# A decoder layer on one core: residuals added in PSUM by an identity matmul, and the first batch's gate projection placed later

## The chip, the cores and the metric

One core of a Trainium2 chip runs the whole program. The metric is the device time of one execution in microseconds (us), where less is better. Times come from repeated runs and from one profiled execution.

## The reference, cut to what matters

The layer works on x of 32 batches x 256 tokens x 256 features. It has three mixers, each followed by a residual and a layer norm. All arithmetic is float32.

```
x = layernorm(x + ssm(x))          # d_inner 512, 16 states, conv of 3 taps
x = layernorm(x + cross_attn(x))   # 16 heads of 16, keys and values from ctx
x = layernorm(x + experts(x))      # 8 experts, d_ff 704, SiLU gate

# ssm, per batch:
xc, res = split(x @ W_in.T + b_in)
u = silu(causal_conv(xc) + conv_b)
dlt, Bm, Cm = split(u @ W_x.T)
delta = softplus(dlt @ W_dt.T + b_dt)
state = exp(delta * A) * state + delta * Bm * u   # a scan over each chunk of 64 tokens
y = sum over states(state * Cm) * silu(res)       # silu(res) is the gate
return y @ W_out.T + b_out
```

## The kernel before

The program has two parts. `mixers` computes the first two layer norms for the 32 batches, `experts` the third. The change touches only `mixers`.

Each engine has its own program, written out by a software pipeline, `run_steps`. A batch's work is cut into pieces, and each piece has an offset. An iteration of the pipeline has 16 slots. A piece with offset o runs in slot o mod 16, and it works on the batch that is o // 16 behind the newest. Within a slot an engine runs its pieces in the order in which its list has them. So in one iteration the convolution of one batch, the scan of the batch before it and the attention of two to five batches before it are interleaved, and an engine that waits in one piece holds up all pieces behind it.

The names that the prediction uses, with the slot of each piece before the change:

- `conv(m)`, m = 0 to 3, on TensorE in slots 1, 3, 5 and 7: the input projection and the convolution, six matmuls of 128x256 from `w_conv`. The PSUM bank `a_ps` holds two of the four blocks, and a bias matmul opens the bank. `conv_evac` on ScalarE (slots 4 and 8) copies the bank to `u`.
- `gate_proj(m)` on TensorE in slots 2 and 6 (bank `f_ps`), and `gate_evac` on ScalarE.
- `silu` on ScalarE (slot 9): a table load, SiLU of `u`, SiLU of the gate, and a second table load. Then `x_proj` (slot 9), `xp_evac`, `dt_proj` (slot 10), `softplus` (slot 11), and on GpSimd `w_piece`, the product of u and delta (slot 12). `delta` and `w` go to DRAM and come back replicated over the partitions.
- The scan: `dBu_piece(t)` on GpSimd, `decay(t, half)` on ScalarE, `scan(t, half)` on VectorE, for 16 tiles t, one per slot. Three `dBu` buffers and three PSUM banks `dA_ps` couple the engines. Some products with C run on GpSimd (`hC_piece`, L516), some on VectorE (L777, followed by `clear_starts`, a small memset, L787, which releases the buffers).
- `state_sum(m)` on TensorE in slots 5, 9, 13 and 1 (bank `y_ps`), after the `hC` products; `gating(m)` on VectorE.
- `out_proj` on TensorE (slot 4) and `attn_out` (slot 0), both into `a_ps`. `residual` on VectorE (slots 5 and 1): one 128x512 add (L804), two `bn_stats` (L807), two aggregations (L813). `norm` on ScalarE (slots 5 and 2).
- The attention, with one head per slot: `scores` and `row_max`; `scores_T` and `softmax_exp`. `head_transpose` on TensorE is in slots 15, 3, 7 and 11, and on its list it stands behind `conv`. `head_norm` on VectorE (L849, L854) is in slots 0, 4, 8 and 12, between the two scans of its slot.

Nine pieces share `a_ps` besides the convolution: `x_proj`, half of `dt_proj`, the projections of q and k, `out_proj`, `attn_out` and three transposes. `Bank.wait_read` makes TensorE wait until the last reader of the bank is done:

```
def wait_read(self, eng):
    if self.last:
        sem, count = self.last
        eng.wait_ge(sem, count)
```

Of the kernel before, what the change touches and what calls it, by code (L numbers as in the profile page):

```python
# [10 lines left out]
ALU = mybir.AluOpType  # L11
# [3 lines left out]
P = 128  # L15
# [4 lines left out]
ND = DI // P  # L20
# [20 lines left out]
NDA = 3  # L41
# [152 lines left out]
def mixers(nc, io, x2_dram, scratch, shared):  # L194
# [3 lines left out]
    with ExitStack() as ctx:  # L198
# [75 lines left out]
        def scores_T_bank(n):  # L274
# [4 lines left out]
        s_const = sem("weights_loaded")  # L279
        s_const_p = sem("const_set_pool")  # L280
# [18 lines left out]
        s_r1, s_st1, s_mv1, s_ln1 = sem("residual1"), sem("stats1"), sem("moments1"), sem("ln1_steps")  # L299
# [15 lines left out]
        s_r2, s_st2, s_mv2, s_ln2 = sem("residual2"), sem("stats2"), sem("moments2"), sem("ln2_steps")  # L315
# [14 lines left out]
        N_CONV = 6 + NDA + TAPS * KD  # L330
# [7 lines left out]
        def _(sp):  # L338
            sp.dma_start(w_xc.rearrange("p q t -> p (q t)"), io["w_xc"]).then_inc(s_conv_ld, 16)
            sp.dma_start(conv_rows, io["conv_rows"].partition_broadcast(P)).then_inc(s_conv_ld, 16)  # L340
            for tile, name in bias_parts:
                sp.dma_start(tile, io[name]).then_inc(s_bias_ld, 16)
# [184 lines left out]
        def _(act):  # L527

            nc.scalar.preload_act_table_set(EXP_LN)
            act.wait_ge(s_bias_ld, 16 * len(bias_parts))  # L530
            nc.scalar.activation(a_neg[:], a_neg[:], ACT.Exp).then_inc(s_const_a, 1)
# [16 lines left out]

            def silu(b):
                act.wait_ge(s_conv, b.value(2, 2))  # L550
                nc.scalar.activation(u[:], u[:], ACT.Silu).then_inc(s_u, 1)
                act.wait_ge(s_gate, b.value(2, 2))
                nc.scalar.activation(gate[:, b.par], gate[:, b.par], ACT.Silu).then_inc(s_gsilu, 1)
                nc.scalar.preload_act_table_set(EXP_LN)

# [33 lines left out]
            def norm(i, s_mv, s_steps, s_x):  # L589
                def piece(b):  # L590
# [101 lines left out]
            def max_load(gr):  # L692
# [11 lines left out]
                *[(O_GATE + 4 * half + 2, gate_evac(half)) for half in range(2)],  # L704
# [20 lines left out]
        def _(dve):  # L725
            nc.vector.memset(xT[:, :, 0:TAPS - 1], 0.0).then_inc(s_const_v, 1)
            nc.vector.memset(eps, EPS).then_inc(s_const_v, 1)
            for i in range(NDA):
                nc.vector.memset(dA[i][:], 0.0).then_inc(s_const_v, 1)
            dve.wait_ge(s_conv_ld, 32)  # L730
# [700 lines left out]
```

## Time and profile before

| | |
|---|---|
| median of 3 runs | 2796.05 us (2788.73 to 2799.86) |
| the profiled execution | 2792.28 us |
| its span, first to last instruction | 2790.5 us |
| busy share TensorE / VectorE / ScalarE / GpSimd | 87% / 77% / 65% / 74% |
| mean granted TensorE clock | 0.955 of full speed |

The span has three stretches. The first 71 us prepare constants and bring batch 0 to its scan. The 32 scans follow, until about 2190 us, and the experts take the rest, with GpSimd idle. Busy shares over the whole span mix these stretches, so the rows below look into one of them at a time. In the timelines, a float32 matmul appears as two instructions, so "x12" is six matmuls.

### The profile page before, as it was taken

To read this page: it belongs to the slowest core of one execution; us is meant where nothing else is said; L and a number is where in the kernel's file an instruction comes from. 1 tells how busy PE (TensorE), PEld (TensorE's weight loads), DVE (VectorE), ACT (ScalarE), POOL (GpSimd) and SP (SyncE) were. 2 spreads that over 40 slices of the span, in tenths; PEclk is the share of its full clock that TensorE was granted. 3 is DMA by queue.
4 is the path that set the end of the run, shared out by engine and by line. 5 is a ranking of instruction groups with operands and counts; after the bars stand their busy time and mean duration, and the time that the engine had idled before them with its cause. 6 is when DMAs were issued, how large, how long until landed. Compare 5 with 4: busy or idle time off the path is not lost. (4 is left out here: it accounts for less than half of the span.)

```text
span 2790.5 us, 49779 instructions
## 1 busy us (share of the span) xinstructions
PE 2424.6 (87%) x14816; PEld 1660.6 (60%) x14816; DVE 2140.0 (77%) x3586; ACT 1802.9 (65%) x3972; POOL 2074.5 (74%) x968
## 2 busy tenths in 40 slices
PE   3578888888889898889889888898888879999998
PEld 2345666666666666666666666666665545555554
DVE  1778999999999999999999999999999832322332
ACT  1666777877888888777877787878777541211111
POOL 2999999999999999999999999999999500000000
PEclk8788999999999999999999999999998879999999
DMA  3456566666666666666666666666666360343221
GB/s 118 128 133 149 150 165 168 165 158 157 157 169 166 160 158 165 165 162 168 166 169 164 162 164 166 165 173 163 166 172 158 86 180 12 91 126 96 78 79 31
DMA packets 319323, 399.65 MB, mean 143 GB/s; under 512 B 115697, under 2 KB 256241, under 8 KB 314962
## 3 DMA queue, kind: packets, MB, share of 16 engines
q1 hardware_dynamic: 303698, 384.91, 53.5%
q10 hardware_dynamic: 15360, 11.55, 1.5%
q8 instruction: 124, 2.03, 0.3%
q14 instruction: 141, 1.16, 0.2%
HBM read 300.86 MB, written 94.37 MB: 142 GB/s over the span
## 5 line engine op out<-in xcount | busy, mean ns | idle before, releaser
L506 POOL TENSOR_TENSOR arena<-arena 128x1024 f32<-128x1024 f32 x512 | 1208.2, 2363 | 66.6 <-DMA arena<-w_dram 42.3
L582 ACT ACTIVATE dA_ps<-arena,a_neg 128x252 f32<-128x252 f32 x2048 | 868.7, 461 | 330.4 <-DVE dA_ps L787 172.0
L764 DVE TENSOR_TENSOR_SCAN arena<-dA_ps,arena 128x512 f32<-128x512 f32 x672 | 803.6, 1208 | 112.5 <-ACT dA_ps L582 88.0
L516 POOL TENSOR_TENSOR arena<-arena 128x1024 f32<-128x1024 f32 (+1 forms) x416 | 808.1, 1943 | 17.8 <-DVE arena L764 17.2
L764 DVE TENSOR_TENSOR_SCAN dA_ps<-dA_ps,arena 128x512 f32<-128x512 f32 x352 | 416.2, 1205 | 3.9 <-POOL arena L506 3.7
L887 PE MATMUL a_ps<-xT,w_conv 128*128 128x256 f32 x1536 | 369.8, 391 | 0.0
L829 DVE TENSOR_REDUCE mx<-s_ps 128x2 f32<-128x512 f32 x497 | 334.0, 672 | 23.2 <-PE s_ps L887 23.2
L887 PEld LDWEIGHTS a_ps<-xT,w_conv 128*128 128x128 f32 x1536 | 288.4, 194 | 54.1 <-issue 16.5
L887 PE MATMUL y_ps<-arena,sel 128*32 128x256 f32 x4096 | 257.5, 393 | 55.5 <-DVE m_rows L835 27.8
L640 ACT ACTIVATE probs<-st_ps 128x512 f32<-128x512 f32 x493 | 285.3, 579 | 29.7 <-PE st_ps L887 25.5
L887 PE MATMUL s_ps<-k_st,q_st 96*128 96x256 f32 x994 | 260.6, 344 | 43.7 <-DVE mx L829 28.0
L887 PE MATMUL st_ps<-q_st,k_st 96*128 96x256 f32 x986 | 221.9, 307 | 51.5 <-ACT probs L640 41.8
L777 DVE TENSOR_TENSOR arena<-dA_ps,arena 128x512 f32<-128x512 f32 x352 | 230.9, 677 | 4.4
L887 PEld LDWEIGHTS st_ps<-q_st,k_st 96*128 96x128 f32 x986 | 154.1, 194 | 120.1 <-issue 100.3
L887 PEld LDWEIGHTS s_ps<-k_st,q_st 96*128 96x128 f32 x994 | 166.7, 197 | 98.0 <-issue 59.4
L887 PEld LDWEIGHTS y_ps<-arena,sel 128*32 128x32 f32 x4096 | 127.9, 112 | 144.2 <-POOL arena L516 64.9
L1240 DVE TENSOR_TENSOR hT<-silu,u_ps 128x512 f32<-128x512 f32 x80 | 55.0, 688 | 193.7 <-PE u_ps L1311 160.9
L887 PE MATMUL a_ps<-bias 2*128 2x512 f32 (+2 forms) x192 | 93.3, 486 | 117.4 <-DVE parts L819 38.4
L1213 ACT ACTIVATE silu<-g_ps 128x512 f32<-128x512 f32 (+1 forms) x96 | 56.5, 596 | 210.0 <-PE g_ps L1311 209.9
L1311 PE MATMUL g_ps<-arena 128*128 128x512 f32 x384 | 181.7, 599 | 3.1 <-PEq L198 3.1
L1311 PE MATMUL u_ps<-arena 128*128 128x512 f32 x320 | 150.5, 592 | 0.0
L1329 PE MATMUL d_ps<-arena,hT 128*128 128x256 f32 x640 | 145.9, 383 | 0.0
(111 smaller groups left out, 3272.9 us busy)
## 6 DMA issues: line engine op xcount, KB each, us to landing
arena<-delta_dram SPq DMA_DIRECT2D x512, 128.0 KB, 2.8
arena<-w_dram SPq DMA_DIRECT2D x512, 128.0 KB, 3.2
arena<-bc_dram SPq DMA_DIRECT2D x128, 256.0 KB, 4.5
q_st<-q_parts_dram SPq DMA_DIRECT2D x512, 64.0 KB
k_st<-k_parts_dram SPq DMA_DIRECT2D x512, 64.0 KB
w_dram<-u SPq DMA_DIRECT2D x32, 512.0 KB, 2.8
delta_dram<-delta SPq DMA_DIRECT2D x32, 512.0 KB, 3.8
k_parts_dram<-parts SPq DMA_DIRECT2D x32, 512.0 KB, 4.0
```

The source lines that it names most:

```text
L506: pool.tensor_tensor(dBu[:, n % NB], w_r[:, n // RP % 2, t % RP].unsqueeze(1).to_broadcast([P, QS, L]), bc_r[:, b.par, 0], ALU.mult).then_ ...
L516: pool.tensor_tensor(h[:, n % NH, states], h[:, n % NH, states], bc_r[:, b.par, 1, states], ALU.mult).then_inc(s_hC, 1)
L582: last = nc.scalar.activation(dA[n % NDA][:, q, :, 1:], delta_r[:, n // (2 * RP) % 2, t % RP].rearrange("p (c t) -> p c t", t=CH)[:, :, 1: ...
L640: nc.scalar.activation(probs[:, n % NPROB], scores_T_bank(n), ACT.Exp, scale=float(DK) ** -0.5).then_inc(s_exp, 1)
L764: nc.vector.tensor_tensor_scan(dst, decays, dBu[:, n % NB, 2 * half:2 * half + 2].rearrange("p q t -> p (q t)"), 0.0, ALU.mult, ALU.add).t ...
L777: nc.vector.tensor_tensor(h[:, n % NH, 2 * half:2 * half + 2], state[:].rearrange("p q c t -> p q (c t)"), bc_r[:, b.par, 1, 2 * half:2 * ...
L829: nc.vector.tensor_reduce(mx[:, hd], scores_bank(b.value(H, hd)), AX.X, ALU.max).then_inc(s_max, 1)
L887: return nc.tensor.matmul(out, lhsT, rhs, start=first, stop=last)
L1213: nc.scalar.activation(dst, g_ps[i % 2][first:last], ACT.Silu).then_inc(f_silu, 1)
L1240: nc.vector.tensor_tensor(hT[first:last, i // 2, HALF * (i % 2):HALF * (i % 2 + 1)], silu[first:last, i % 2], ups[first:last], ALU.mult).t ...
L1311: ins = nc.tensor.matmul(ps[i % 2][:], w13[:, b.par, k, col:col + P], x2T[:, b.par, k, cols], start=(k == 0), stop=(k == KD - 1))
L1329: nc.tensor.matmul(d_ps[(2 * t + i) % ND_PS][:, 0:D], hT[:, k, tokens], w2[:, b.par, k], start=(k == 0), stop=False)
```

## The change

1. The two residual adds leave VectorE. After the matmuls of `out_proj` and of `attn_out`, TensorE multiplies the identity by the tokens' x and accumulates into the same bank: one 128x256 matmul per 128 tokens, so two for each projection. `bn_stats` and the normalisation read the sum from `a_ps`, no longer from SBUF.
2. The bank `a_ps` is therefore released by the last read of `norm` on ScalarE, where it was released by the add.
3. `conv(0)` moves on TensorE from slot 1 to slot 3, and `conv(2)` from slot 5 to slot 7. Each bank of the convolution is now opened and filled in one slot.
4. For batch 0 only, the gate projection moves behind `dt_proj`, and its copies and SiLU behind `softplus`. `x_proj` waits for three weights that are loaded first.
5. At the start, the bias rows are loaded ahead of the convolution weights, and ScalarE copies them instead of VectorE.

```diff
-            (w_gate[:], "w_gate"), (w_x[:], "w_x"), (w_dt[:], "w_dt"), (sel[:], "sel"), (w_out[:], "w_out"),
+        front_weights = [(w_x[:], "w_x"), (w_dt[:], "w_dt"), (w_gate[:], "w_gate")]
...
+            for tile, name in bias_parts:
+                sp.dma_start(tile, io[name]).then_inc(s_bias_ld, 16)
             sp.dma_start(w_xc.rearrange("p q t -> p (q t)"), io["w_xc"]).then_inc(s_conv_ld, 16)
...
             def load_weights():
+                for tile, name in front_weights:
+                    sp.dma_start(tile, io[name]).then_inc(s_front, 16)
+                sp.wait_ge(s_const_v, N_SET)
                 for tile, name in weights:
                     sp.dma_start(tile, io[name]).then_inc(s_const, 16)
-                    sp.wait_ge(s_const_v, N_SET)
...
+            act.wait_ge(s_const_v, N_ROWS)
+            nc.scalar.activation(bias[:], rows, ACT.Copy).then_inc(s_const_a, 1)
...
+            def silu_gate(b):
+                act.wait_ge(s_gate, b.value(2, 2))
+                nc.scalar.activation(gate[:, b.par], gate[:, b.par], ACT.Silu).then_inc(s_gsilu, 1)
+
             def silu(b):
                 act.wait_ge(s_conv, b.value(2, 2))
                 nc.scalar.activation(u[:], u[:], ACT.Silu).then_inc(s_u, 1)
-                act.wait_ge(s_gate, b.value(2, 2))
-                nc.scalar.activation(gate[:, b.par], gate[:, b.par], ACT.Silu).then_inc(s_gsilu, 1)
+                if b.back(1):
+                    silu_gate(b)
                 nc.scalar.preload_act_table_set(EXP_LN)
+
+            def first_gate(b):
+                if not b.back(1):
+                    for half in range(2):
+                        gate_evac(half)(b)
+                    silu_gate(b)
+                    nc.scalar.preload_act_table_set(EXP_LN)
...
-                        nc.scalar.activation(xt[:, b.c % NX, tt], xt[:, b.c % NX, tt], ACT.Identity, bias=shift[:, i, tt:tt + 1],
+                        nc.scalar.activation(xt[:, b.c % NX, tt], a_ps[:, tt], ACT.Identity, bias=shift[:, i, tt:tt + 1],
                                              scale=rstd[:, i, tt:tt + 1]).then_inc(s_x, 1)
...
-                *[(O_GATE + 4 * half + 2, gate_evac(half)) for half in range(2)],
+                *[(O_GATE + 4 * half + 2, later_gate_evac(half)) for half in range(2)],
+                (O_SP + 2, first_gate),
...
-            def residual(i, s_mm, src_ps, s_r, s_st, s_mv, s_steps, s_in, per_batch):
-                def piece(b):
-                    r = xt[:, b.c % NX]
+            def moments(i, s_mm, s_st, s_mv, s_steps):
+                def piece(b):
                     dve.wait_ge(s_mm, b.value(TT, TT))
-                    dve.wait_ge(s_in, b.value(per_batch, per_batch))
-                    nc.vector.tensor_tensor(r, src_ps[:], r, ALU.add).then_inc(s_r, 1)
-                    dve.wait_ge(s_r, b.value(1, 1))
                     for tt in range(TT):
-                        nc.vector.bn_stats(st[:, i, tt], r[:, tt]).then_inc(s_st, 1)
+                        nc.vector.bn_stats(st[:, i, tt], a_ps[:, tt]).then_inc(s_st, 1)
...
+            def first_gate(b):
+                if not b.back(1):
+                    for m in range(ND):
+                        gate_proj(m)(b)
...
             def x_proj(b):
+                if not b.back(1):
+                    pe.wait_ge(s_front, 16 * len(front_weights))
+                    pe.wait_ge(s_const_v, N_SET)
...
                     for k in range(ND):
-                        i = mm(a_ps[:, tt, :], g[:, k, tt * P:(tt + 1) * P], w_out[:, k], False,
-                               tt == TT - 1 and k == ND - 1)
-                    i.then_inc(s_out_mm, 1)
-                    bank_a.read_by(s_r1, 1, b, 1)
+                        mm(a_ps[:, tt, :], g[:, k, tt * P:(tt + 1) * P], w_out[:, k], False, False)
+                    if tt == 0:
+                        pe.wait_ge(s_xtok, b.value(16, 16))
+                    mm(a_ps[:, tt, :], ident[:], x_of(b)[:, tt], False, tt == TT - 1).then_inc(s_out_mm, 1)
+                    bank_a.read_by(s_x1, TT, b, TT)
...
+                    mm(a_ps[:, tt, :], ident[:], x_of(b)[:, tt], False, tt == TT - 1).then_inc(s_of_mm, 1)
+                    bank_a.read_by(s_x2, TT, b, TT)
...
-                *[(O_CONV + 2 * m, conv(m)) for m in range(ND)],
-                *[(O_GATE + 4 * (m // 2), gate_proj(m)) for m in range(ND)],
+                *[(O_CONV + 2 + 4 * (m // 2), conv(m)) for m in range(ND)],
+                *[(O_GATE + 4 * (m // 2), later_gate(m)) for m in range(ND)],
+                (O_SP + 1, first_gate),
```

**The first place** is TensorE's program in slots 3 and 4 of an iteration in the middle of the run. `s_ps` and `st_ps` are `scores` and `scores_T`, and `f_ps<-ident,oT` is `head_transpose`. Before:

```order
L887 MATMUL s_ps<-k_st,q_st 128x256 x2
L887 MATMUL st_ps<-q_st,k_st 128x256 x2
L887 MATMUL a_ps<-xT,w_conv 128x256 x6
L1084 MATMUL f_ps<-ident,oT 128x128 x2
L887 MATMUL s_ps<-k_st,q_st 128x256 x2
L887 MATMUL st_ps<-q_st,k_st 128x256 x2
L887 MATMUL a_ps<-bias 128x512
L887 MATMUL a_ps<-w_out,g 128x256 x8
```

And of the change:

```order
L906 MATMUL s_ps<-k_st,q_st 128x256 x2
L906 MATMUL st_ps<-q_st,k_st 128x256 x2
L906 MATMUL a_ps<-bias 128x512
L906 MATMUL a_ps<-xT,w_conv 128x256 x12
L1117 MATMUL f_ps<-ident,oT 128x128 x2
L906 MATMUL s_ps<-k_st,q_st 128x256 x2
L906 MATMUL st_ps<-q_st,k_st 128x256 x2
L906 MATMUL a_ps<-bias 128x512
L906 MATMUL a_ps<-w_out,g 128x256 x4
L906 MATMUL a_ps<-x_tok,ident 128x256
L906 MATMUL a_ps<-w_out,g 128x256 x4
L906 MATMUL a_ps<-x_tok,ident 128x256
```

Twelve convolution matmuls and a bias now stand ahead of `head_transpose`, where there were six. Two identity matmuls stand in `out_proj`.

**The second place** is TensorE in slots 5 to 7 of the same iteration. `f_ps<-probs,v` is the product of probabilities and values, and `y_ps<-arena,sel` is `state_sum`. Before:

```order
L887 MATMUL f_ps<-probs,v 32x256 x8
L887 MATMUL a_ps<-bias 128x512
L887 MATMUL a_ps<-xT,w_conv 128x256 x6
L887 MATMUL s_ps<-k_st,q_st 128x256 x2
L887 MATMUL y_ps<-arena,sel 32x256 x16
L887 MATMUL st_ps<-q_st,k_st 128x256 x2
L887 MATMUL f_ps<-bias 128x512
L887 MATMUL f_ps<-xT,w_gate 128x256 x4
L887 MATMUL s_ps<-k_st,q_st 128x256 x2
L887 MATMUL st_ps<-q_st,k_st 128x256 x2
L887 MATMUL a_ps<-xT,w_conv 128x256 x6
L1084 MATMUL f_ps<-ident,oT 128x128 x2
```

And of the change:

```order
L906 MATMUL f_ps<-probs,v 32x256 x8
L906 MATMUL s_ps<-k_st,q_st 128x256 x2
L906 MATMUL y_ps<-arena,sel 32x256 x16
L906 MATMUL st_ps<-q_st,k_st 128x256 x2
L906 MATMUL f_ps<-bias 128x512
L906 MATMUL f_ps<-xT,w_gate 128x256 x4
L906 MATMUL s_ps<-k_st,q_st 128x256 x2
L906 MATMUL st_ps<-q_st,k_st 128x256 x2
L906 MATMUL a_ps<-bias 128x512
L906 MATMUL a_ps<-xT,w_conv 128x256 x12
L1117 MATMUL f_ps<-ident,oT 128x128 x2
```

The six matmuls of `conv(2)` and the bias have left the place behind `probs,v` and stand directly ahead of `conv(3)` and `head_transpose`.

**The third place** is the start of TensorE's program, batch 0. Before:

```order
L887 MATMUL a_ps<-bias 128x512
L887 MATMUL a_ps<-xT,w_conv 128x256 x6
L887 MATMUL f_ps<-bias 128x512
L887 MATMUL f_ps<-xT,w_gate 128x256 x4
L887 MATMUL a_ps<-xT,w_conv 128x256 x6
L887 MATMUL a_ps<-bias 128x512
L887 MATMUL a_ps<-xT,w_conv 128x256 x6
L887 MATMUL f_ps<-bias 128x512
L887 MATMUL f_ps<-xT,w_gate 128x256 x4
L887 MATMUL a_ps<-xT,w_conv 128x256 x6
L887 MATMUL a_ps<-u,w_x 96x256 x4
L887 MATMUL a_ps<-xp,w_dt 128x256 x2
```

And of the change:

```order
L906 MATMUL a_ps<-bias 128x512
L906 MATMUL a_ps<-xT,w_conv 128x256 x12
L906 MATMUL a_ps<-bias 128x512
L906 MATMUL a_ps<-xT,w_conv 128x256 x12
L906 MATMUL a_ps<-u,w_x 96x256 x4
L906 MATMUL a_ps<-xp,w_dt 128x256 x2
L906 MATMUL f_ps<-xp,w_dt 128x256 x2
L906 MATMUL f_ps<-bias 128x512
L906 MATMUL f_ps<-xT,w_gate 128x256 x4
L906 MATMUL f_ps<-bias 128x512
L906 MATMUL f_ps<-xT,w_gate 128x256 x4
L906 MATMUL f_ps<-bias 128x512
```

The four blocks of the convolution are no longer interleaved with the gate projection, which now follows `dt_proj`.

## Rows read from the trace of the kernel before

**Rows 1.** The page's first part, busy time of an engine (share of the span)
```profile
PE 2424.6 (87%) x14816; PEld 1660.6 (60%) x14816; DVE 2140.0 (77%) x3586; ACT 1802.9 (65%) x3972; POOL 2074.5 (74%) x968
```

**Rows 2.** windows: start:end length, PE, PEld, DVE, ACT, POOL busy, clock, DMA
```profile
140.00:210.00 70.00, 52.37 (x302) 34.86 (x294) 53.43 (x74) 43.31 (x93) 68.64 (x33) 0.85 0.56 133
...
1400.00:1750.00 350.00, 311.31 (x2185) 224.12 (x2184) 324.66 (x533) 277.87 (x627) 337.55 (x159) 0.98 0.65 164
```

**Rows 3.** what GpSimd waited for between 400 and 2000 us
```profile
POOL arena L506 <- DMA arena<-w_dram: 23.3, 22, 2.8
POOL arena L506 <- DVE dA_ps L787: 14.8, 40, 1.3
POOL arena L516 <- DVE arena L764: 13.8, 39, 1.0
```

**Rows 4.** groups of instructions by line and shape, 400 to 2000 us
```profile
L506 POOL TENSOR_TENSOR arena<-arena 128x1024 f32<-128x1024 f32 x384 | 906.1, 2363 | 38.6 <-DMA arena<-w_dram 23.3 <-DVE dA_ps L787 14.8
...
L887 PE MATMUL a_ps<-xT,w_conv 128*128 128x256 f32 x1152 | 269.5, 383 | 0.0
...
L807 DVE BATCH_NORM_STATS2 st<-x_tok 128x6 f32<-128x256 f32 x96 | 36.2, 419 | 1.6
...
L804 DVE TENSOR_TENSOR x_tok<-a_ps,x_tok 128x512 f32<-128x512 f32 x48 | 32.6, 680 | 32.4 <-PE a_ps L887 32.4
```

**Rows 5.** timeline of TensorE in one batch: start, length, xcount
```profile
1004.89 0.50 PE L887 MATMUL a_ps<-bias 16*128 16x512 f32 x1
1005.32 2.86 PE L887 MATMUL a_ps<-xT,w_conv 128*128 128x256 f32 x12
...
1008.42 1.93 PE L887 MATMUL y_ps<-arena,sel 128*32 128x256 f32 x32
...
1013.49 2.76 PE L887 MATMUL a_ps<-xT,w_conv 128*128 128x256 f32 x12
1016.08 0.38 PE L1084 MATMUL f_ps<-ident,oT 128*128 128x128 f32 x2
...
1031.75 2.76 PE L887 MATMUL a_ps<-xT,w_conv 128*128 128x256 f32 x12
1034.34 0.38 PE L1084 MATMUL f_ps<-ident,oT 128*128 128x128 f32 x2
```

**Rows 6.** timeline of VectorE in the same batch
```profile
1016.58 0.18 DVE L849 RECIPROCAL rsum<-f_ps 128x8 f32<-128x8 f32 x1
...
1021.18 0.69 DVE L804 TENSOR_TENSOR x_tok<-a_ps,x_tok 128x512 f32<-128x512 f32 x1 [1.25 <-PE a_ps L887]
...
1034.77 0.20 DVE L849 RECIPROCAL rsum<-f_ps 128x8 f32<-128x8 f32 x1
```

**Rows 7.** timeline of ScalarE in the same batch
```profile
1016.28 0.60 ACT L538 ACTIVATE u<-a_ps 128x512 f32<-128x512 f32 x1
...
1029.91 0.47 ACT L582 ACTIVATE dA_ps<-arena,a_neg 128x252 f32<-128x252 f32 x1 [3.09 <-DVE dA_ps L787]
```

**Rows 8.** timeline of GpSimd in the same batch
```profile
1006.03 2.34 POOL L516 TENSOR_TENSOR arena<-arena 128x1024 f32<-128x1024 f32 x1
...
1036.50 2.37 POOL L516 TENSOR_TENSOR arena<-arena 128x1024 f32<-128x1024 f32 x1
```

**Rows 9.** timeline of all engines, the first 71 us
```profile
15.73 5.49 PE L887 MATMUL a_ps<-xT,w_conv 128*128 128x256 f32 x12
...
31.63 3.65 PE L887 MATMUL f_ps<-xT,w_gate 128*128 128x256 f32 x8
...
47.50 1.28 ACT L551 ACT_TABLE_LOAD   x1
48.79 1.06 ACT L551 ACTIVATE u<-u 128x1024 f32<-128x1024 f32 x1
...
56.36 2.34 POOL L497 TENSOR_TENSOR u<-u,delta 128x1024 f32<-128x1024 f32 x1 [43.11 <-ACT delta L572]
...
70.65 6.96 POOL L506 TENSOR_TENSOR arena<-arena 128x1024 f32<-128x1024 f32 x3 [11.96 <-DMA arena<-w_dram]
```

More of the change, by code:

```diff
@@ L279, in mixers @@
         s_const = sem("weights_loaded")
+        s_front = sem("front_weights_loaded")
         s_const_p = sem("const_set_pool")
@@ L329, in mixers @@
         N_WEIGHTS = len(weights)
-        N_CONV = 6 + NDA + TAPS * KD
+        N_ROWS = 3 + NDA
+        N_CONV = 5 + NDA + TAPS * KD
         N_SET = N_CONV + 2
@@ L551, in silu, with later_gate_evac @@
                 nc.scalar.activation(u[:], u[:], ACT.Silu).then_inc(s_u, 1)
-                act.wait_ge(s_gate, b.value(2, 2))
-                nc.scalar.activation(gate[:, b.par], gate[:, b.par], ACT.Silu).then_inc(s_gsilu, 1)
+                if b.back(1):
+                    silu_gate(b)
                 nc.scalar.preload_act_table_set(EXP_LN)
+            def first_gate(b):
[4 more added lines that the diff above has]
+                    nc.scalar.preload_act_table_set(EXP_LN)
+            def later_gate_evac(half):
+                def piece(b):
+                    if b.back(1):
+                        gate_evac(half)(b)
+                return piece
             def xp_evac(b):
@@ L729, in _ @@
                 nc.vector.memset(dA[i][:], 0.0).then_inc(s_const_v, 1)
+            dve.wait_ge(s_bias_ld, 16 * len(bias_parts))
+            nc.vector.tensor_tensor(rows, rows, row_scales, ALU.mult).then_inc(s_const_v, 1)
             dve.wait_ge(s_conv_ld, 32)
@@ L734, in _ @@
                                             conv_rows[:, tap * DI:(tap + 1) * DI], ALU.mult).then_inc(s_const_v, 1)
-            dve.wait_ge(s_bias_ld, 16 * len(bias_parts))
-            nc.vector.tensor_tensor(rows, rows, row_scales, ALU.mult).then_inc(s_const_v, 1)
-            dve.wait_ge(s_const_v, N_CONV - 3)
-            nc.vector.tensor_copy(bias[:], rows).then_inc(s_const_v, 1)
-            dve.wait_ge(s_const_v, N_CONV - 2)
+            dve.wait_ge(s_const_a, 1)
             for first, last, cols in ((0, 96, BC), (96, P, 2 * BC)):
@@ L905, in piece @@
                     pe.wait_ge(s_xT, b.value(16, 16))
-                    if m == 0 and not b.back(1):
-                        pe.wait_ge(s_const, 16 * N_WEIGHTS)
-                        pe.wait_ge(s_const_v, N_SET)
-                        pe.wait_ge(s_const_p, 4)
                     if m % 2 == 0:
@@ L918, in gate_proj, with later_gate, piece @@
                 return piece
+            def first_gate(b):
+                if not b.back(1):
+                    for m in range(ND):
+                        gate_proj(m)(b)
+            def later_gate(m):
+                def piece(b):
+                    if b.back(1):
+                        gate_proj(m)(b)
+                return piece
             def x_proj(b):
+                if not b.back(1):
+                    pe.wait_ge(s_front, 16 * len(front_weights))
+                    pe.wait_ge(s_const_v, N_SET)
                 pe.wait_ge(s_u, b.value(1, 1))
@@ L940, in piece @@
                     n = b.value(NU, 4 * m)
+                    if m == 0 and not b.back(1):
+                        pe.wait_ge(s_const, 16 * N_WEIGHTS)
+                        pe.wait_ge(s_const_p, 4)
                     pe.wait_ge(s_hC, b.value(len(HC_POOL), sum(t < 4 * m + 4 for t in HC_POOL)))
@@ L1097, in piece @@
                     for k in range(KD):
-                        i = mm(a_ps[:, tt, :], onT[:, k, tt * P:(tt + 1) * P], w_o[:, k], False,
-                               tt == TT - 1 and k == KD - 1)
-                    i.then_inc(s_of_mm, 1)
-                    bank_a.read_by(s_r2, 1, b, 1)
+                        mm(a_ps[:, tt, :], onT[:, k, tt * P:(tt + 1) * P], w_o[:, k], False, False)
+                    mm(a_ps[:, tt, :], ident[:], x_of(b)[:, tt], False, tt == TT - 1).then_inc(s_of_mm, 1)
+                    bank_a.read_by(s_x2, TT, b, TT)
                 return piece
```

13 lines of the change are left out of this document (6 added, 7 removed).

## The prediction

> **What bounds the kernel now.** I read the page first. Over the whole span TensorE looks busiest, at 87% [rows 1], but that mixes the scans with the experts. The windows separate them. In the middle of the scans (1400 to 1750 us) GpSimd is busy 337.55 of 350 us, VectorE 324.66, TensorE 311.31, and the granted clock is 0.98, which is the upper level of 2.4 GHz nearly all the time [rows 2]. So GpSimd sets the pace, and the view to read next is what it waits for.
>
> A batch has 16 of the L506 products. 384 of them stand in the 1600 us from 400 to 2000 [rows 4], so that window holds 24 batches and a batch takes 66.7 us. In it GpSimd waits 23.3 us for replicated data, and 14.8 and 13.8 us for VectorE [rows 3]. That is 52 us, or 2.2 us per batch. If the change made every other engine free, it could win only these 2.2 us per batch. This is the first thing to see: taking work from VectorE has a ceiling of about 60 us in all.
>
> The second thing is that GpSimd leads only by a little. I followed one batch, from 1000 to 1067 us. The `state_sum` of slot 1 starts on TensorE at 1008.42 [rows 5], just behind the GpSimd product that begins at 1006.03 and takes 2.34 us, to 1008.37 [rows 8]. Slot 2's work follows and the block `conv(1)` of slot 3 runs from 1013.49 to 1016.25. The head transpose ends at 1016.46 [rows 5], ScalarE copies the bank at 1016.28 [rows 7], and VectorE's head norm starts at 1016.58 [rows 6]. VectorE then waits 1.25 us for `out_proj` and adds at 1021.18. It works without a gap until a memset (L787) for which ScalarE has waited 3.09 us; the decay behind it starts at 1029.91 [rows 7]. Its softmax then lets TensorE go, and `conv(3)` starts at 1031.75. The head transpose of slot 7 ends at 1034.72 [rows 5], and VectorE wants it at 1034.77 [rows 6]. One scan later, at 1036.50, GpSimd starts the product that needs that scan [rows 8]. From there GpSimd paces until the next batch's slot 1. This is a closed loop through all four engines, with slacks of about 0.1 us at its hand-offs. What is added to TensorE on this loop is paid, although the busy share of TensorE shows 11% of room.
>
> **The change part by part.** Prices first. 1152 convolution instructions take 269.5 us, 0.234 us each, and a float32 matmul of 128x256 is two of them: 0.47 us [rows 4]. A block of the convolution takes 2.76 us, and its bias holds TensorE 0.43 us (1004.89 to 1005.32) [rows 5].
>
> *The adds.* Off VectorE go two adds per batch, of 0.68 us each [rows 4]. On TensorE come two identity matmuls ahead of each of the two hand-offs, 0.93 us. At `attn_out` VectorE did not wait in this batch. It gains up to 0.68 us there, but the gain is lost again, since TensorE's slot 2 starts after a `state_sum` that waits for GpSimd [rows 5, 8]. At `out_proj` VectorE was waiting already (32.4 us in all at L804, 1.3 us per batch) [rows 4]. So there the loop becomes longer by 0.93 and shorter by 0.68: +0.25 us.
>
> *Statistics and normalisation from PSUM.* No row has `bn_stats` on PSUM. From SBUF it takes 0.419 us for 256 columns, and the add reads PSUM at 0.680 us for 512 columns, 0.34 us per 256 [rows 4]. I take 0.42 us, no change; the bounds are 0.34 and, if the fixed part is all of the difference, 0.68 us, which would be -0.2 to +0.5 us per pair. The normalisation on ScalarE keeps its count; a PSUM read of 512 columns takes 0.60 us there [rows 7]. I cost it at nothing, because it runs while ScalarE has 3 us of waiting ahead (the 3.09 us) [rows 7]. Without that cover it would be some 0.1 us.
>
> *The bank held longer.* `a_ps` is now free only after `norm`. The convolution of slot 3 asks for it at about 1013.5, where the statistics of slot 1 are long done, so I see no wait. In the Trainium skill, the page "PSUM — Partial Sum Buffer" (section "Summary: rules for kernel authors") advises to evacuate PSUM promptly, because it is small. That speaks against this change, and by the page alone the longer hold would be the cost. By the timeline the hold itself costs nothing; what was rearranged to make room for it costs.
>
> *The move of the convolution* is the large part. Before, `conv(0)` ran from 1004.89 to 1008.18, ahead of a `state_sum` that could not begin before GpSimd's product ended at 1008.37 [rows 5, 8]. It was free. Now it stands in slot 3, and a slot of TensorE from 1008.42 on has no hole. The second block and the bias come ahead of the head transpose: 2.76 + 0.43 = 3.19 us. Queued behind them on TensorE are the transpose, `scores` and `out_proj`, on ScalarE everything behind the copy of the bank (decays, softmax), and on VectorE `scan(t, 1)` behind the head norm. `conv(2)` is the same again. It leaves slot 5, where VectorE then was the one waited for, and enters slot 7, directly ahead of the transpose that VectorE takes 0.05 us after its end [rows 5, 6]: 3.19 us. The slacks I subtract are 0.12 us (1016.46 to 1016.58) and 0.05 us.
>
> Per iteration: 3.19 + 3.19 + 0.25 - 0.17 = 6.5 us. It needs iterations with both a convolution and head transposes in slots 3 and 7. Those are the iterations 4 to 31, 28 of them. Sum 28 x 6.5 = 182 us. Before iteration 4 GpSimd is busy 68.64 of 70 us while VectorE has 16 us of room [rows 2], so I cost those at nothing; with that cover gone it would be four more times 6.5 us, 26 us.
>
> *Batch 0.* Before, TensorE did the first block from 15.73 to 21.22 and then waited; the gate projection started at 31.63, and SiLU of u at 48.79, ending at 49.85 [rows 9]. Now the four blocks run without the gate. The first is done at 21.22, the second 2.76 to 5.49 us later by the two lengths that stand in the rows. Copy 0.60 [rows 7], bias 0.43, two blocks 5.5, copy 0.6, and a table load of 1.28 and the SiLU of 1.06 us [rows 9] end at 33.5 to 36.2, so 13.6 to 16.3 us earlier. The rest of the path, 49.85 to GpSimd's 56.36 and on to 70.65, stays [rows 9]. I take 15 us. The gate work then hides in the 12 us (11.96) that GpSimd waits for DMA [rows 9]. The order of the constants changes nothing: all the same bytes must land, and the same products follow.
>
> **Sum.** 2792.3 - 15 + 182 = 2959 us. The profiled execution is 3.8 us below the median of the runs, well inside their 11 us, so I leave the sum there and say 2958.
>
> **The rivals.**
> - *Faster, since GpSimd is the bound and the rest absorbs.* It is for this that VectorE is 7% idle and TensorE 11%. Then the start gives 15 us, and fewer waits on VectorE up to (14.8 + 13.8) / 24 = 1.2 us per batch, 33 us in 28: between 2744 and 2777 us. Against it stand the hand-offs without slack. It decides if TensorE can begin slot 3 about 3 us ahead of where it does now, and slot 7 too. Chance 0.16.
> - *One move costs and the other is absorbed.* 28 x 3.3 = 92 us, less 15: about 2870. For it: VectorE's gain at `attn_out`, and GpSimd's own 2.2 us of waits, which could shrink. Chance 0.17.
> - *Both cost, and TensorE slows down too.* With periods of 73 us and the same work, TensorE is busy about 84%. Where it is busy 52.37 of 70 us, the granted clock is 0.85 [rows 2]. About 20 us per batch of the loop are TensorE's. A clock of 0.9 makes these 1.6 us longer, 45 us in all: about 3003. The page "TensorE: Matmul & The Clock Gate" (section "HAM oscillation — how this bites in real kernels") says that an engine with idle gaps falls back to the slower clock; this is the rule behind this rival, and the traces of the early windows agree with it. Chance 0.09.
> - *No measurable change*: gain at the start offset by some absorbed stalls. Chance 0.03.
> - The forecast, both moves paid at the full clock: chance 0.55, from 2925 to 2985.
>
> **How the numbers follow.** The range 2860 to 3000 holds the forecast and the second case and leaves out the faster one, no change and the upper part of the slowest, about 2 in 10. From the cases: faster by over 0.5% 0.16, within 0.5% 0.03, slower 0.81. Half a per cent, 14 us, is about what a measurement of this kernel can tell from no change.
>
> **What would show it.** GpSimd's share in the window 1400 to 1750 falls from 96% to about 88%, with new waits for VectorE of 6 us per batch. VectorE waits at the head norm for the transposes of slots 3 and 7, about 3 us each, and about 2 us at its statistics behind `out_proj`. ScalarE waits about 3 us at both copies of the convolution. TensorE has a hole ahead of the `state_sum` of slot 1. The first L506 comes at about 56 us. Wrong would be a period that stays near 66.7 us, or a wait of TensorE ahead of the convolution for ScalarE's `norm`, which I put at zero.

## The result, and the profile after

The changed kernel takes 3011.83 us (median of 4 runs, 3000.85 to 3020.74) where the kernel before takes 2792.94 us in the same comparison. It is slower by the factor 1.0778, with a 95% interval of 1.0756 to 1.0800. The direction was as forecast (2958 us) and the size was 54 us short; the time lies 12 us above the range of 2860 to 3000. The profiled execution took 3011.76 us, with a span of 3009.9 us and a mean granted clock of 0.940.

The page's first part and the window from 1400 to 1750 us, in the columns of [rows 2]:

```profile
PE 2537.6 (84%) x15072; PEld 1734.9 (58%) x15072; DVE 2100.2 (70%) x3521; ACT 1800.9 (60%) x3975; POOL 2075.7 (69%) x968
```

and the window:

```profile
1400.00:1750.00 350.00, 295.93 (x1974) 213.05 (x1965) 279.29 (x458) 247.17 (x551) 298.75 (x141) 0.96 0.54 143
```

GpSimd, which set the pace with 337.55 of 350 us [rows 2], is busy 298.75 us. No engine is near its limit now, so the waits must tell. The waits between 400 and 2000 us (who waited for whom: us in total, times, longest), GpSimd's (in this kernel L787 is VectorE's scan and L810 the memset, and L511 and L521 are GpSimd's two products):

```profile
POOL arena L521 <- DVE arena L787: 105.9, 50, 4.6
POOL arena L511 <- DVE dA_ps L810: 88.9, 82, 2.2
```

VectorE's:

```profile
DVE rsum L868 <- PE f_ps L1117: 150.1, 46, 4.1
DVE st L826 <- PE a_ps L906: 49.0, 33, 2.2
```

ScalarE's:

```profile
ACT u L545 <- PE a_ps L906: 145.1, 42, 4.0
```

and TensorE's:

```profile
PE s_ps L906 <- DVE mx L848: 98.9, 83, 2.5
PE y_ps L906 <- POOL arena L521: 33.0, 37, 1.2
```

GpSimd waits 194.8 us for VectorE, where it waited 14.8 + 13.8 = 28.6 [rows 3]. The same 1600 us hold 21.5 batches here and 24 there, so that is 9.1 us per batch in place of 1.2. VectorE waits at the head norm, which takes the transposes of slots 3 and 7, 150.1 / 46 = 3.3 us each time. ScalarE waits 145.1 / 42 = 3.5 us at each copy of the convolution.

One batch shows the order of it. TensorE's timeline (start, length, in brackets the idle time before it and what ended it):

```profile
1030.02 0.47 PE L906 MATMUL s_ps<-k_st,q_st 96*128 96x256 f32 x2 [1.05 <-DVE mx L848]
1031.38 1.93 PE L906 MATMUL y_ps<-arena,sel 128*32 128x256 f32 x32 [0.88 <-POOL arena L521]
...
1036.49 0.49 PE L906 MATMUL a_ps<-bias 16*128 16x512 f32 x1
1036.91 5.45 PE L906 MATMUL a_ps<-xT,w_conv 128*128 128x256 f32 x24
1042.20 0.38 PE L1117 MATMUL f_ps<-ident,oT 128*128 128x128 f32 x2
...
1051.89 0.47 PE L906 MATMUL s_ps<-k_st,q_st 96*128 96x256 f32 x2 [2.18 <-DVE mx L848]
```

VectorE's, over the same stretch:

```profile
1042.62 0.21 DVE L868 RECIPROCAL rsum<-f_ps 128x8 f32<-128x8 f32 x1 [3.01 <-PE f_ps L1117]
...
1048.16 0.76 DVE L826 BATCH_NORM_STATS2 st<-a_ps 128x6 f32<-128x256 f32 x2 [2.17 <-PE a_ps L906]
```

and ScalarE's:

```profile
1042.40 0.60 ACT L545 ACTIVATE u<-a_ps 128x512 f32<-128x512 f32 x1 [2.47 <-PE a_ps L906]
```

In slot 1 TensorE now has holes of 1.05 and 0.88 us and in slot 5 one of 2.18 us, where the blocks of the convolution had been. In slot 3 the two blocks end only at 1042.36. ScalarE has waited 2.47 us for that end and VectorE 3.01 us for the transpose behind it, and then 2.17 us for `out_proj`.

**Where the 219 us are.** The windows from one `w_piece` of GpSimd to the next are one batch each. Of the kernel before:

```profile
180.16:245.39 65.23, 49.40 (x290) 34.89 (x288) 54.90 (x80) 41.77 (x92) 64.18 (x31) 0.87 0.71 158
314.97:381.69 66.72, 58.08 (x415) 41.59 (x414) 62.08 (x102) 53.18 (x120) 64.56 (x30) 1.00 0.66 160
582.25:648.15 65.90, 58.29 (x419) 42.08 (x418) 61.73 (x102) 53.63 (x121) 64.47 (x30) 1.00 0.66 166
2053.08:2119.09 66.01, 58.41 (x419) 42.07 (x418) 61.80 (x102) 53.52 (x121) 64.49 (x31) 1.00 0.67 165
```

Of the changed kernel:

```profile
171.92:247.60 75.68, 53.34 (x294) 37.11 (x292) 54.20 (x78) 41.79 (x92) 64.20 (x31) 0.82 0.60 137
326.01:402.19 76.18, 64.64 (x423) 46.30 (x422) 61.17 (x100) 52.74 (x120) 64.49 (x30) 0.93 0.59 141
1150.30:1222.19 71.89, 60.43 (x427) 43.76 (x426) 60.64 (x100) 53.42 (x121) 64.51 (x30) 1.00 0.59 153
1222.19:1300.08 77.89, 66.40 (x427) 47.29 (x426) 60.75 (x100) 53.43 (x121) 64.53 (x31) 0.91 0.52 141
2266.00:2338.05 72.05, 60.30 (x427) 43.69 (x426) 60.64 (x100) 53.36 (x121) 64.56 (x31) 1.00 0.59 151
```

The third window of before and the third of after have the clock at 1.00: 65.90 and 71.89 us, a difference of 6.0 us. From 314.97 to 2119.09 there are 27 batches of 66.82 us on average, and from 326.01 to 2338.05 there are 27 of 74.52 us. So the average lies 0.92 us above the full-clock batch before and 2.63 us above it after. At a clock of 0.91 a batch takes 77.89 us.

`w_piece` stands in slot 12, and the first head transposes of slots 3 and 7 in iteration 4. So the first three windows hold what comes before iteration 4, and the fourth already holds one of the 28 iterations of the prediction's sum. The first three took 189.0 us (56.36 to 245.39) and take 206.1 us (41.50 to 247.60). The fourth took 69.58 us and takes 78.41. The sum of the spans' difference:

| part | us |
|---|---|
| start (41.50 in place of 56.36) | -14.9 |
| first three batches, ahead of iteration 4 | +17.1 |
| 28 batches at full clock, 6.0 us each | +168 |
| 28 batches, time above the full-clock length, 1.75 us each | +49 |
| the rest of the program | +0.5 |
| together (3009.9 - 2790.5) | +219.4 |

The start itself, in the rows that answer to [rows 9]:

```profile
32.29 1.06 ACT L562 ACTIVATE u<-u 128x1024 f32<-128x1024 f32 x1
...
33.60 3.62 PE L906 MATMUL a_ps<-u,w_x 128*96 128x256 f32 x8 [3.26 <-ACT u L562]
...
41.50 2.35 POOL L502 TENSOR_TENSOR u<-u,delta 128x1024 f32<-128x1024 f32 x1 [28.26 <-ACT delta L596]
...
55.32 6.96 POOL L511 TENSOR_TENSOR arena<-arena 128x1024 f32<-128x1024 f32 x3 [11.47 <-DMA arena<-w_dram]
```

### The profile page after: what moved, and what is told of

Same layout as the page of the kernel before. It is cut to its first block and busy times, and to the rows that moved or that the text cites. A ratio compares the mean times of both kernels' runs of the same rounds, so it can differ in the third digit from the quotient of the medians.

```text
span 3009.9 us, 50166 instructions
## 1 busy us (share of the span) xinstructions
PE 2537.6 (84%) x15072; PEld 1734.9 (58%) x15072; DVE 2100.2 (70%) x3521; ACT 1800.9 (60%) x3975; POOL 2075.7 (69%) x968
## 5 line engine op out<-in xcount | busy, mean ns | idle before, releaser
L511 POOL TENSOR_TENSOR arena<-arena 128x1024 f32<-128x1024 f32 x512 | 1208.0, 2361 | 167.2 <-DVE dA_ps L810 135.4
L521 POOL TENSOR_TENSOR arena<-arena 128x1024 f32<-128x1024 f32 (+1 forms) x416 | 807.3, 1941 | 147.9 <-DVE arena L787 147.9
L787 DVE TENSOR_TENSOR_SCAN arena<-dA_ps,arena 128x512 f32<-128x512 f32 x672 | 803.3, 1208 | 98.6 <-ACT dA_ps L606 71.2
L787 DVE TENSOR_TENSOR_SCAN dA_ps<-dA_ps,arena 128x512 f32<-128x512 f32 x352 | 416.3, 1205 | 5.4 <-POOL arena L511 3.7
L906 PE MATMUL y_ps<-arena,sel 128*32 128x256 f32 x4096 | 282.0, 421 | 81.6 <-POOL arena L521 75.9
L906 PE MATMUL a_ps<-xT,w_conv 128*128 128x256 f32 x1536 | 350.5, 384 | 0.0
L906 PEld LDWEIGHTS y_ps<-arena,sel 128*32 128x32 f32 x4096 | 134.1, 117 | 179.8 <-POOL arena L521 84.9
L868 DVE RECIPROCAL rsum<-f_ps 128x8 f32<-128x8 f32 x128 | 25.5, 199 | 220.8 <-PE f_ps L1117 220.8
L545 ACT ACTIVATE u<-a_ps 128x512 f32<-128x512 f32 x64 | 38.2, 596 | 234.3 <-PE a_ps L906 234.3
```

What stands on the lines that cost most here:

```text
L511: pool.tensor_tensor(dBu[:, n % NB], w_r[:, n // RP % 2, t % RP].unsqueeze(1).to_broadcast([P, QS, L]), bc_r[:, b.par, 0], ALU.mult).then_ ...
L521: pool.tensor_tensor(h[:, n % NH, states], h[:, n % NH, states], bc_r[:, b.par, 1, states], ALU.mult).then_inc(s_hC, 1)
L787: nc.vector.tensor_tensor_scan(dst, decays, dBu[:, n % NB, 2 * half:2 * half + 2].rearrange("p q t -> p (q t)"), 0.0, ALU.mult, ALU.add).t ...
L906: return nc.tensor.matmul(out, lhsT, rhs, start=first, stop=last)
```

## The experiments

The ratios are to the kernel before, run on the same chip, with their 95% interval. The medians are of 4 to 7 runs.

| kernel | median us | ratio |
|---|---|---|
| changed kernel | 3011.83 | 1.0778 (1.0756 to 1.0800) |
| start alone | 2781.22 | 0.9950 (0.9934 to 0.9966) |
| moved convolution alone | 3112.55 | 1.1142 (1.1121 to 1.1163) |
| changed, convolution in its old slots | 3036.12 | 1.0864 (1.0845 to 1.0883) |
| changed, holes filled | 2959.39 | 1.0594 (1.0576 to 1.0612) |
| moved convolution alone, holes filled | 2980.65 | 1.0671 (1.0655 to 1.0687) |
| one block moved | 2935.34 | 1.0516 (1.0498 to 1.0533) |
| changed, transposes first | 3185.97 | 1.1397 (1.1341 to 1.1454) |
| changed, transposes and scores first | 3190.53 | 1.1423 (1.1393 to 1.1453) |
| changed, transposes between the blocks | 3035.26 | 1.0880 (1.0850 to 1.0910) |
| start alone, `x_proj` twice | 2780.81 | 0.9959 (0.9943 to 0.9976) |

### The start alone

The kernel before with parts 4 and 5 of the change; adds, bank and convolution slots are the old ones.

> The kernel before with parts 4 and 5 of the change alone (batch 0's gate work behind its softplus, the front weights and bias rows first); adds and convolution slots as before. If the start gains what it gained in the changed kernel (first scan product of GpSimd at 55.3 us where it was 70.7) and nothing else follows from it, the time is 15 us shorter than before, about 2778 us, ratio 0.995. Rival: the gain at the start is given back as the stages settle into the same phase, so within 3 us of before.

It takes 2781.22 us against 2797.02 of the kernel before beside it, 15.8 us less. The rival falls: the gain at the start is kept to the end. This is also the version that beats both kernels, the kernel before by half a per cent.

### The moved convolution alone

```diff
-                *[(O_CONV + 2 * m, conv(m)) for m in range(ND)],
+                *[(O_CONV + 2 + 4 * (m // 2), conv(m)) for m in range(ND)],
```

> The kernel before with one edit: the first two convolution blocks both in slot 3, the last two both in slot 7. Theory: this move alone makes the loss. A batch then takes about 71.8 us at full clock and 74.4 on average, and the early batches lose 26 us, so the time is about 3020 us (the changed kernel plus its 15 us of start). Rival 1: the identity matmuls and the longer hold of the bank are the cost; then this stays within 20 us of before. Rival 2: half each, about 2900 us.

Both rivals fall: the move by itself makes a loss, even a larger one than that of the whole change. It takes 3112.55 us, 92 us more than expected. The reason is in the window of one of its batches and in TensorE's timeline:

```profile
1044.30:1122.81 78.51, 66.16 (x419) 46.18 (x418) 62.00 (x102) 53.80 (x121) 64.51 (x30) 0.89 0.53 140
```

and the timeline:

```profile
1068.76 0.76 PE L887 MATMUL s_ps<-k_st,q_st 96*128 96x256 f32 x2 [2.19 <-DVE mx L829]
...
1074.47 3.78 PE L887 MATMUL f_ps<-xT,w_gate 128*128 128x256 f32 x8
...
1093.98 0.47 PE L887 MATMUL s_ps<-k_st,q_st 96*128 96x256 f32 x2 [2.90 <-DVE mx L829]
...
1098.53 3.76 PE L887 MATMUL f_ps<-xT,w_gate 128*128 128x256 f32 x8
```

The clock is 0.89 in this batch. Behind the hole of 2.19 us in slot 1 and that of 2.90 us in slot 5 the gate projections take 3.78 and 3.76 us. The window of the first and that of another one later in this run give the level, in the column of the clock:

```profile
1074.47:1078.25 3.78, 3.78 (x10) 3.06 (x10) 0.66 (x1) 1.53 (x4) 3.78 (x2) 0.50 0.94 290
1846.92:1848.91 1.99, 1.99 (x11) 1.77 (x10) 1.99 (x5) 1.25 (x3) 1.99 (x2) 1.00 0.99 282
```

At 0.50, the lower level (1.2 GHz), the eight instructions take 3.78 us; at 1.00, the upper one (2.4 GHz), they take 1.99 us. Of the gate projections that start between 400 and 2030 us, 25 of 42 take over 3 us here, 16 of 44 in the changed kernel and none of 49 in the kernel before. TensorE's longest hole between 400 and 2000 us is 3.54 us here, 2.54 us in the changed kernel and 1.36 us in the kernel before.

### The old slots with the bank held

```diff
-                *[(O_CONV + 2 + 4 * (m // 2), conv(m)) for m in range(ND)],
+                *[(O_CONV + 2 * m, conv(m)) for m in range(ND)],
```

> The changed kernel with the convolution blocks back in slots 1, 3, 5 and 7, while the bank is still held until the normalisation has read it. If holding the bank costs nothing, this is 2780 us plus 0.25 us per batch, about 2790 us. Theory: it does cost, because the first block in slot 1 must wait for the normalisation in slot 2 of ScalarE, which ends about 5 us later than the block began before, and the block in slot 5 the same; TensorE then starts slot 2 about 5 us late, so 5 us or more per batch, 2920 to 3050 us, with waits of TensorE ahead of the convolution bias for ScalarE.

3036.12 us, within the range of the theory. What TensorE waits for, and the first block in one batch:

```profile
PE a_ps L906 <- ACT x_tok L627: 137.4, 42, 4.5
```

in the timeline:

```profile
1020.55 0.47 PE L906 MATMUL a_ps<-bias 16*128 16x512 f32 x1 [4.18 <-ACT x_tok L627]
1020.95 4.54 PE L906 MATMUL a_ps<-xT,w_conv 128*128 128x256 f32 x12
```

TensorE waits for the normalisation that reads `a_ps`, 137.4 us in 42 waits, 4.18 us ahead of this block. So the hold of the bank is not free. Either the first block waits for the normalisation, or it is moved out of the way, and the second is only 24 us cheaper. The clock falls here too: the block behind this hole takes 4.54 us, with a granted clock of 0.62, where it took 2.86 [rows 5], and no batch of this run from the fifth on has a clock above 0.95.

### The holes filled

```diff
                     bank_f.wait_read(pe)
+                    if gr in (1, 2) and b.c >= 0:
+                        for k in range(FILL):
+                            mm(f_ps[:, 1, :], w_conv[:, 0, 0, 0:P], w_conv[:, 1, 0, 0:L], k == 0, k == FILL - 1)
                     for kt in range(TT):
```

> The changed kernel with work added that nobody reads: four float32 matmuls of 128x256 into the free half of f_ps ahead of the products of probabilities and values in slots 1 and 5, 1.9 us each, where the convolution blocks had stood. Clock theory: TensorE's granted clock falls since it idles there, and this costs 1.7 us per batch; with the holes filled the clock returns to about 0.97 and the time falls by 20 to 50 us, to 2960 to 2990 us, although the kernel does more. Rival: the holes are not what lowers the clock; then the added 3.7 us per batch are hidden or paid, and the time is the same or up to 100 us longer.

The kernel does eight float32 matmuls more per batch (16 instructions; 3.4 us: 63.81 against 60.43 busy) and takes 52 us less. A batch of it:

```profile
1046.07:1117.96 71.89, 63.81 (x443) 46.49 (x442) 60.63 (x100) 53.35 (x121) 64.52 (x30) 1.00 0.59 152
```

TensorE is busier (63.8 of 71.9 us) and the clock is 1.00. Its longest hole between 400 and 2000 us is 1.41 us, and none of its 45 gate projections takes over 3 us. The batch is as long as the changed kernel's at full clock, and the 27 batches take 72.46 us on average in place of 74.52. The waits at the head norm and at the copies stay (139.8 us in 48 and 136.9 us in 44). So the filler costs nothing, it leaves the price of the move as it was, and the clock was what the long batches had lost.

### The moved convolution alone, holes filled

The same filler in the kernel with the moved convolution alone.

> The kernel with the moved convolution alone (3112 us), with the same filler as before: four matmuls that nobody reads in slots 1 and 5. Clock theory: the move's own price is 6 us per batch, and the other 6.5 us at a mean clock of 0.89 come from the gate projections run at the lower level behind the holes. With the holes filled a batch takes about 72 us, the mean clock in the scans is back at 0.97 or more, and the time is the filled changed kernel (2959) plus its 15 us of start, about 2975 us. Rival: the adds on VectorE are what makes this kernel slower than the changed one; then it stays above 3050 us.

2980.65 us. The filler takes 132 us off, and the rival falls. One of 44 gate projections takes over 3 us. A batch at full clock takes 72.20 us:

```profile
1143.63:1215.83 72.20, 62.28 (x435) 44.95 (x434) 61.90 (x102) 53.76 (x121) 64.59 (x31) 1.00 0.57 152
```

This also prices the adds, together with the longer hold of the bank, which no run separates from them. With the holes filled in both, the kernel with the old adds is slower by 1.0671 - 1.0594 - 0.0050 (its start) = 0.0027 of 2793 us, 7 us. The three intervals together leave about 8 us on either side of that, so by the times alone it could be nothing. The profiles are finer: ten full-clock batches take 72.20 to 72.22 us here and eleven take 71.88 to 71.90 us in the filled changed kernel, which is 0.3 us per batch in favour of the adds on TensorE. With the holes open the same subtraction, 1.1142 - 1.0778 - 0.0050 = 0.0314, gives 88 us. The other 81 us go together with the clock, which is 0.904 in the one span and 0.940 in the other.

### One block moved

```diff
-                *[(O_CONV + 2 * m, conv(m)) for m in range(ND)],
+                *[(O_CONV + (2 if m == 0 else 2 * m), conv(m)) for m in range(ND)],
```

> The kernel before with one block moved, the first, from slot 1 to slot 3; the third stays in slot 5. Theory of two separate hand-offs: half the price, 3.1 us per batch at full clock and up to 3 us more for the hole in slot 1, plus 13 us in the early batches, 2890 to 2975 us. Rival: the stages have room for one move and the loss comes only from both together; then within 30 us of before.

2935.34 us, and one of its batches at full clock:

```profile
1975.27:2044.43 69.16, 58.40 (x419) 42.13 (x418) 61.86 (x102) 53.55 (x121) 64.52 (x30) 1.00 0.62 159
```

69.16 us is 3.26 us over 65.90; two blocks moved are 6.30 us over it (72.20, in the filled kernel, since no batch of the unfilled one has the full clock). So one block costs half of what two cost, and the rival falls. The other block was not moved by itself.

### Transposes first, and scores too

The head transposes ahead of the convolution in TensorE's list; in the second kernel the scores of slots 3 and 7 as well.

```diff
+                *[(O_ON + HG * gr, head_transpose(gr)) for gr in range(NG)],
                 *[(O_CONV + 2 + 4 * (m // 2), conv(m)) for m in range(ND)],
...
-                *[(O_ON + HG * gr, head_transpose(gr)) for gr in range(NG)],
```

> The changed kernel with the head transposes ahead of the convolution on TensorE's list. Nothing is added or removed. Theory A: the price of the move is VectorE's wait at the head norm; without it 4 to 6 us per batch come back, 2850 to 2900 us. Theory B: ScalarE's copy of the bank and out_proj behind it hang on the same end of the convolution, so VectorE only waits elsewhere (scores, statistics); less than 2 us per batch come back, 2955 to 3012 us.

> As the run with the transposes first, and the scores of slots 3 and 7 ahead of the convolution too, so that VectorE waits for nothing behind it except the statistics after out_proj. Theory A: all of the 6 us come back, about 2830 us. Theory B: ScalarE still stands 3 us at each copy of the convolution, and out_proj is as late as before; at most half comes back, 2920 to 2990 us.

Both theories missed: 3185.97 and 3190.53 us, 174 and 179 us more than the changed kernel. The edit made new waits. The larger of them in the first of the two kernels, and its place in one batch:

```profile
PE f_ps L1117 <- ACT gate L553: 59.5, 39, 2.1
PE f_ps L1117 <- ACT delta L596: 33.5, 20, 1.7
```

in the timeline of TensorE:

```profile
1012.82 0.41 PE L1117 MATMUL f_ps<-ident,oT 128*128 128x128 f32 x2 [1.27 <-ACT gate L553]
```

The transpose writes `f_ps`, which in slot 2 took the gate projection; ScalarE's copy of that reads the bank in slot 4. With the convolution ahead of it the transpose came after this copy. Now TensorE waits for the copy, and the convolution waits behind. The second row is the same at the transpose that meets softplus's reads of `f_ps`. Together they are 4.7 us per batch, and the changed kernel has neither. The mean clock is lower too, 0.911 against 0.940, and how the loss divides between the two was not measured. The runs say nothing on theories A and B.

### Transposes between the blocks

```diff
+                *[(O_CONV + 2 + 4 * (m // 2), conv(m)) for m in (0, 2)],
+                *[(O_ON + HG * gr, head_transpose(gr)) for gr in (1, 2)],
+                *[(O_CONV + 2 + 4 * (m // 2), conv(m)) for m in (1, 3)],
```

> The changed kernel with the head transposes of slots 3 and 7 between the two blocks of the convolution, so at the same distance behind its start as in the kernel before, and those of slots 11 and 15 where they were. The scores, ScalarE's copy and out_proj stay behind both blocks. Theory A: VectorE's wait at the head norm makes the price; then 4 to 6 us per batch come back, 2850 to 2900 us. Theory B: the end of the second block releases ScalarE's copy and out_proj too, and these carry the same delay; VectorE's wait moves to the scores and statistics, at most 1 us per batch comes back at full clock, 2975 to 3015 us.

3035.26 us, 23 us over the changed kernel by the medians and 20 us over the range of theory B. Theory A falls, and theory B forecast the place of the waits but not the time. VectorE's waits in this kernel:

```profile
DVE mx L848 <- PE s_ps L906: 85.3, 64, 4.5
DVE st L826 <- PE a_ps L906: 80.4, 28, 3.7
DVE m_rows L854 <- ACT m_rows L702: 53.9, 21, 2.6
DVE rsum L868 <- PE f_ps L1117: 48.4, 43, 1.6
```

The head norm waits 48.4 us where it waited 150.1. The scores take 85.3 and the statistics 80.4 us in its place. This fits the view that the end of the second block is what everything hangs on: curing the wait at the top of the list moves it to the next in line. Why the kernel became slower, and not equal, I did not settle. Its full-clock batches take 72.35 us against 71.89, and its 27 batches 75.36 against 74.52 on average, so about half of the 23 us is there at full clock.

### x_proj twice

```diff
-                for k in range(ND):
+                for k in [*range(ND), *range(ND)]:
                     i = mm(a_ps[0:RANK + 2 * NS, 0, :], w_x[:, k], u[:, k], k == 0, k == ND - 1)
```

> The kernel with the new start alone (2781 us), with x_proj computed twice into the same place, four float32 matmuls more per batch (1.9 us), ahead of three waits of TensorE of about 1.1 us each in slots 9 to 12. A batch of the kernel before takes 65.9 us where the clock is full and 66.8 us on average. Clock theory: with shorter holes the clock falls less often, up to 0.9 us per batch come back, 2755 to 2780 us. Rival: the added work is on the path to softplus, 0.5 us per batch longer, 2780 to 2800 us.

0.9959 against 0.9950 for the start alone: no difference that can be measured. 1.9 us of work per batch fits in here for nothing, which shows that TensorE has room in slots 9 to 12 while it had none in slots 3 and 7. The mean clock of the runs is 0.960 against 0.957, and no time follows from it.

## Why the prediction was wrong

The path and the price of the move held. Two terms that the sum put at nothing failed: the clock (49 us) and the batches before iteration 4 (17 us). The move itself came out 14 us below its 182 us.

- **GpSimd sets the pace by little, and a loop through four engines has no slack.** Right. After the change all engines have idle time and the period is longer. GpSimd's share falls to 85% (88% forecast), and its waits for VectorE grow by 7.9 us per batch (6 forecast).
- **The move of the convolution, 3.19 us per block.** Right, and shown by the run with one block: 3.26 us, and 6.30 us for two. All 28 iterations cost 168 us at full clock, 6.0 us each, where the sum had 6.5. The places were the ones named: 3.3 us at the head norm, 3.5 us at ScalarE's copy (3 us forecast), 2.17 us at the statistics behind `out_proj` (2 us forecast).
- **The adds, +0.25 us per batch.** Small, but the sign was wrong. The difference of the full-clock batches with the holes filled is 72.20 - 71.89 = 0.31 us in their favour, some 8 us in all; the times of the runs say 7 us, which is within their noise. VectorE's own work in a batch falls to 60.6 us from 61.8, and I had written off the part at `attn_out`. Against the +0.25 of the sum that is 0.56 us, about the whole difference between 6.5 and 6.0.
- **Statistics from PSUM at the same price.** Right, by the changed kernel's groups of instructions (busy time, mean ns of one | idle time before them):

```profile
L627 ACT ACTIVATE x_tok<-a_ps,shift,rstd 128x256 f32<-128x256 f32 x86 | 43.0, 549 | 0.0
...
L826 DVE BATCH_NORM_STATS2 st<-a_ps 128x6 f32<-128x256 f32 x86 | 32.7, 421 | 49.3 <-PE a_ps L906 49.0
```

0.421 us where it was 0.419 [rows 4]. The normalisation takes 0.549 us from PSUM, and took 0.586 us from SBUF in the kernel before.
- **The bank held longer costs nothing.** Right for the changed kernel, where no wait of TensorE for the normalisation shows. But the run with the old slots shows that this hold is what makes the move necessary, at 4.18 us and 2.31 us of waits. The rule of the Trainium skill, "PSUM — Partial Sum Buffer", section "Summary: rules for kernel authors", to evacuate PSUM promptly, is borne out by these waits; what they show is a bank that other pieces stand in line for, and not a lack of memory, which is the section's reason. I had separated the hold from the move, and so made its cost look like that of something else.
- **The batches before iteration 4, at nothing.** This term failed: 17.1 us, 10.5 of them in the third batch (75.68 us in place of 65.23). I had two reasons for nothing. One was that a loss needs the head transposes, and they are absent from that batch. But the scores stand behind the convolution as well, and ScalarE's copy does. The waits of the third batch, in the changed kernel:

```profile
DVE mx L848 <- PE s_ps L906: 10.2, 4, 3.6
ACT u L545 <- PE a_ps L906: 8.5, 2, 4.7
```

and in the kernel before:

```profile
DVE mx L829 <- PE s_ps L887: 1.6, 2, 1.3
ACT u L538 <- PE a_ps L887: 1.5, 1, 1.5
```

The other reason was the cover of GpSimd, judged by its busy share over 70 us. In this batch it waits 8.7 us for VectorE's memset, and waited 0.6 us before. I named 26 us as the price with the cover gone, for four batches; 17 came in three. The run with the moved convolution alone loses 14.2 us in the same three batches, so most of the loss comes with the move. How the 17 us divide between these waits and the clock (0.82 in the third batch, 0.87 before) stays open; with the holes filled 14.4 are left.
- **The clock.** This is the larger failed term, 49 us. With the holes filled the batches lie 0.57 us above the full-clock length and no longer 2.63, so nearly all of it goes with the clock. The sum took the full clock throughout and left the clock to a rival with a chance of 0.09, at 3003 us. That rival is the case that came, but the closeness of its number is in part luck. It had a clock of 0.9 on 20 us of each batch (which from 0.98 is nearer 1.8 us than the 1.6 written there). The mean clock of the 27 batches was 0.96 where it had been 0.98, and it cost as much. Its total also lacks the early batches and has the move 14 us too dear, and these two nearly cancel. It reasoned from the busy share, however, and not from the holes: I had said in the same text that `conv(0)` leaves time which TensorE must wait out, and did not ask what the emptied time does. The filled kernels show it: with 52 and 132 us less for more work, the place of the idle time decides. The page "TensorE: Matmul & The Clock Gate" of the Trainium skill (section "HAM oscillation — how this bites in real kernels") ties a lower clock to idle time of the engine. The direction agrees with these traces, where a third of the changed kernel's gate projections run at half speed, although by their size alone the section's rule would have forecast no fall, since it speaks of longer gaps than the 2.54 us that is the longest hole in the changed kernel between 400 and 2000 us. The traces decide, and in them the clock fell. They do not show which holes bring the clock down in one batch and not in the next, and that stays open.
- **The start, -15 us.** Right in its sum: 14.9 us in the profile, 15.8 us in the run with the start alone. Two misses cancel in it. SiLU of u ends at 33.35 us, 16.5 us earlier, just more than the 13.6 to 16.3 forecast. And `x_proj` behind it takes 3.62 us at a clock of 0.53, where it took 1.97 us at 1.00: the path from SiLU to GpSimd did not stay.
- **What decides against the faster rival.** It asked whether TensorE could begin slot 3 about 3 us earlier. It cannot: the `state_sum` of slot 1 still waits for GpSimd (33.0 us in 37 waits).

## What to carry to other kernels

Ask of a piece of work that moves in an in-order list what it leaves behind and what it lands in front of. Here a block left 3 us in which its engine had to wait anyway, and landed ahead of a copy and a transpose that ScalarE and VectorE took up within 0.4 us of its end; a busy share of 89% said nothing about either.

A resource that is held longer is paid by whoever must be moved out of its way. Price the hold and the move as one.

Where TensorE's time is on the path, price the holes that a change opens at the lower clock too.

## What had not been expected of the hardware

Work that nobody reads made the kernel faster: eight float32 matmuls (3.4 us) more per batch, 52 us less in all (1.0594 against 1.0778), and 132 us less with the moved convolution alone (1.0671 against 1.1142). TensorE was busy over 80% of the time in those batches and its longest hole was 2.54 us in the changed kernel and 3.54 us with the moved convolution alone, and yet 16 of 44 gate projections of the one and 25 of 42 of the other ran at half speed. Where the longest holes were 1.36 to 1.82 us (the kernel before and the two filled ones), 1 of 138 did.
